# Key sums of a cross-attention kernel: multiply and add in one VectorE operation, eleven of them inside the first layer

## The reference, cut to what matters

```python
x = x + alpha * (softmax((x @ wq.T) @ (ctx @ wk.T).T / sqrt(512)) @ (ctx @ wv.T)) @ wo.T
for i in (1, 2):                                   # the two layers, H=16, K=128
    h  = layer_norm(x, ln_scale[i], ln_offset[i])
    qh = (h @ wq[i] + bq[i]);  kh = (ctx @ wk[i] + bk[i]);  vh = (ctx @ wv[i] + bv[i])
    kh = concat(kh, bias_k[i]);  vh = concat(vh, bias_v[i])   # position 361
    x  = x + softmax(qh @ kh.T / sqrt(128)) @ vh @ wo[i] + bo[i]
h = layer_norm(x, ...);  x = x + gelu(h @ w_fc1 + b_fc1) @ w_fc2 + b_fc2
```

## Time and profile before

| what | value |
|---|---|
| median of 3 runs | 1841.67 us (1839.01 to 1846.27) |
| the profiled execution | 1845.13 us |
| its span, first to last instruction | 1843.3 us |
| mean granted TensorE clock | 0.995 of full |
| busy: PE, DVE, ACT, POOL | 98%, 61%, 44%, 42% of the span |
| DMA | 123.80 MB, mean 67 GB/s |

### The profile page before, as it was taken

The page is one execution under the profiler, slowest core; times in us unless marked ns, Lnnn a source line. Parts: engine busy times, 40 slices in busy tenths (PEclk is TensorE's granted clock), DMA queues, the critical chain, the costliest instruction groups (busy, mean ns, idle before and its releaser), DMA issues.

```text
span 1843.3 us, 30698 instructions
## 1 busy us (share of the span) xinstructions
PE 1814.3 (98%) x11548; PEld 1777.6 (96%) x11548; DVE 1119.8 (61%) x2518; ACT 806.2 (44%) x1868; POOL 773.3 (42%) x634
## 2 busy tenths in 40 slices
PE   8889999999999999999999999999999999999999
PEld 5789999999999999999999999999999999999999
DVE  3676556555575565566688555556666566555565
ACT  3534344434444434344475443444435334434354
POOL 2685252453162352531378245343245252353244
PEclk9999999999999999999999999999999999999999
DMA  8952011111020121210372112121112021111132
GB/s 249 241 172 63 29 53 41 47 58 41 12 76 24 47 59 34 64 31 29 109 227 85 39 47 58 30 58 41 30 52 59 24 62 31 47 58 41 35 100 85
DMA packets 73590, 123.80 MB, mean 67 GB/s; under 512 B 13888, under 2 KB 25536, under 8 KB 73444
## 3 DMA queue, kind: packets, MB, share of 16 engines
q1 hardware_dynamic: 71140, 117.64, 21.8%
q10 hardware_dynamic: 2304, 4.20, 0.7%
HBM read 119.20 MB, written 2.61 MB: 66 GB/s over the span
## 4 chain that ended last, share of the span: by engine, by line
PE 89%; DVE 5%; DMA 2%; ACT 2%; SPq 1%; issue 1%; DVEq 0%; ACTq 0%
PE psum L589 27%; PE psum L590 27%; PE psum L591 27%; PE psum L875 4%; DMA ctxT_in<-ctxT_dram 1%; DVE xT L1536 1%; DMA ctx_rows_in<-ctx_dram 1%; PE psum L750 1%; PE psum L841 1%; DVE h_lo L1342 1%; PE psum L602 1%; PE psum L598 1%; DVE psum L1504 1%; PE psum L599 0%; PE psum L768 0%
## 5 line engine op out<-in xcount | busy, mean ns | idle before, releaser
L471 POOL TENSOR_TENSOR wbuf_hi<-stage,zero_col 128x512 fp32r<-128x512 f32 x256 | 267.5, 1045 | 916.1 <-PE psum L591 545.2
L521 POOL TENSOR_TENSOR wbuf_lo<-stage,wbuf_hi 128x512 fp32r<-128x512 f32 x256 | 329.5, 1287 | 20.1
L589 PE MATMUL psum<-pT_hi,ctx_rows_hi 121*128 121x250 f32 (+3 forms) x1152 | 332.0, 288 | 1.2 <-DVE pT_lo L1338 1.2
L591 PE MATMUL psum<-pT_hi,ctx_rows_lo 121*128 121x250 f32 (+3 forms) x1152 | 332.3, 288 | 0.0
L590 PE MATMUL psum<-pT_lo,ctx_rows_hi 121*128 121x250 f32 (+3 forms) x1152 | 331.1, 287 | 0.0
L589 PE MATMUL psum<-ctxT_hi,a_hi 128*125 128x362 f32 (+1 forms) x832 | 280.5, 337 | 0.0
L1338 DVE TENSOR_TENSOR a_lo<-psum,a_hi 128x500 fp32r<-128x500 f32 (+2 forms) x288 | 146.2, 526 | 210.2 <-ACT a_hi L996 209.5
L591 PE MATMUL psum<-ctxT_hi,a_lo 128*125 128x362 f32 (+1 forms) x832 | 273.2, 328 | 0.0
L590 PE MATMUL psum<-ctxT_lo,a_hi 128*125 128x362 f32 (+1 forms) x832 | 272.9, 328 | 0.0
L589 PE MATMUL psum<-a_hi,wbuf_hi 128*128 128x400 f32 x720 | 254.0, 353 | 0.0
L590 PE MATMUL psum<-a_lo,wbuf_hi 128*128 128x400 f32 x720 | 248.4, 345 | 0.0
(11 more groups left out here) (183 smaller groups left out, 3563.8 us busy)
## 6 DMA issues: line engine op xcount, KB each, us to landing
stage<-head_w_dram SPq DMA_DIRECT2D x256, 256.0 KB, 2.6
mlp_stage<-mlp_w_dram SPq DMA_DIRECT2D x32, 512.0 KB, 3.9
ctx_rows_in<-ctx_dram SPq DMA_DIRECT2D x12, 726.0 KB
ctxT_in<-ctxT_dram SPq DMA_DIRECT2D x12, 724.0 KB, 10.3
key_stage<-head_w_dram SPq DMA_DIRECT2D x32, 256.0 KB, 7.4
l0w<-l_w_dram ACTq DMA_DIRECT2D x16, 256.0 KB, 8.4
kb<-diff_scratch SPq DMA_DIRECT2D x32, 64.0 KB, 4.3
out_dram<-y_out SPq DMA_DIRECT2D x8, 200.0 KB, 2.6
```

Of the source, the lines that this page charges most:

```text
L471: return nc.gpsimd.tensor_tensor(out, in_, zero_col[0:in_.shape[0], :].broadcast_to(tuple(in_.shape)), ALU.add)
L521: nc.gpsimd.tensor_tensor(lo, held, hi.bitcast(F32), ALU.subtract).then_inc(stage_free, 1)
L589: pe.matmul(out, a_h, x_hi, start=start, stop=False)
L591: return pe.matmul(out, a_l, x_hi, start=False, stop=stop)
```

## The change

- A key sum is now four `tensor_tensor_reduce` on DVE, one for each 128 columns, straight from `key_stage` and `kb` (product and sum in one operation). POOL's products and the `kw` buffers are gone.
- Twenty-one sums are done in the single head. The other eleven are done inside steps (0,0) to (1,3) of pass 0, in slot a or b (`LATE_KEYS_AT`), through one pair of buffers, `kb_late` and `key_stage_late`. Their loads stand in SP's list behind the stage loads 8, 12, 14, 15, 17 and 21 (`LATE_KEYS_BEHIND`), and each waits until the sum before it is done.
- `key_parts(0)` stands between centring and inverting of the first norm, where four sums stood; `key_parts(1)` moves from step (0,0) to behind step (3,2).
- The first four pairs of buffers lie over the rows that the `dv_scratch` stores read, so SP waits for `dv_out` before it loads the first keys, and it loads them ahead of `load_ctx_columns(1, 0)`.
- ACT does `exp0(0)` and `exp0(1)` ahead of the splits beside them, and the splits of the context rows of turn 1 come later; DVE does `maxima0(1)` and `maxima0(2)` earlier.
- POOL splits weights 0 to 3 as soon as the 21 sums are done, and clears `dv3`, `pb3` then.

```diff
+KEYS, EARLY_KEYS, KEY_WBUF = 7, 4, 2
+LATE_KEYS_AT = {
+    (0, 0): "b", (0, 1): "ab", (0, 2): "ab", (0, 3): "ab", (1, 0): "b", (1, 1): "b", (1, 2): "b", (1, 3): "b",
+}
+LATE_KEYS_BEHIND = {8: 1, 12: 1, 14: 2, 15: 5, 17: 1, 21: 1}
...
             sp.wait_ge(diff_out, 16)
+            sp.wait_ge(dv_out, 32)
+            some_key_weights(EARLY_KEYS)
             for b in range(3):
                 sp.wait_ge(ls_mm, b + 1)
-                if b == 0:
-                    some_key_weights(4)
                 load_ctx_columns(1, b)
-            some_key_weights(1)
...
-                some_key_weights((2, 2, 1, 5)[b])
+                some_key_weights((1, 2, 1, 2)[b])
...
+                if i < KEYS_BEFORE:
...
+                else:
+                    sp.wait_ge(kw_sum, i)
+                    sp.dma_start(kb_late[:, :], diff_d[i].partition_broadcast(P)).then_inc(late_ld, 16)
+                    sp.dma_start(key_stage_late[:, :], head_w_d[i * 4 + KINDS.index("q")]).then_inc(late_ld, 16)
...
             def key_sums(i):
-                dve.wait_ge(kw_s, i + 1)
-                nc.vector.tensor_reduce(w0[:, :, i], kw[i % len(kw)][:, :, :], AX_X, ALU.add).then_inc(kw_sum, 1)
...
+                for c in range(DC):
+                    summed = nc.vector.tensor_tensor_reduce(
+                        out=chunk(held, c), in0=chunk(held, c), in1=diffs[:, :], scale=1.0, scalar=0.0, op0=ALU.mult,
+                        op1=ALU.add, accum_out=w0[:, c, i:i + 1])
+                summed.then_inc(kw_sum, 1)
...
                 if j == 0:
-                    some_key_sums(4)
+                    key_parts(0)
...
-                        if ph == 0 and before is None:
-                            key_parts(1)
                         run_pieces((k, b, "a"))
+                        if ph == 0 and "a" in LATE_KEYS_AT.get((k, b), ""):
+                            some_key_sums(1)
...
+                    if ph == 0:
+                        some_key_sums("b" in LATE_KEYS_AT.get((k, b), ""))
+                        if (k, b) == (3, 2):
+                            key_parts(1)
```

More of the change, by code:

```diff
@@ L215, in build @@
         dv3 = sb("dv3", [65, 2, 2 * P], F32R)
+        with ExitStack() as before_aside:
+            key_stage_late = sb("key_stage_late", [P, D], F32, before_aside)
+            kb_late = sb("kb_late", [P, P], F32, before_aside)
         aside_hi, aside_lo = split("aside", [P, N])
         with ExitStack() as before_layers:
-            key_stage = sb("key_stage", [P, KEYS, D], F32, before_layers)
+            sb("first_wbufs", [P, KEY_WBUF * 2 * D], F32, before_layers)
+            key_stage += [sb(f"key_stage{j}", [P, D], F32, before_layers) for j in range(EARLY_KEYS, KEYS)]
+        kb = kb_first + kb
         w_hi, w_lo = zip(*[split(f"wbuf{j}", [P, D]) for j in range(WBUFS)])
@@ L551, in _ @@
                             pool.wait_ge(n_lo, n_chunks(BETWEEN, 0, DC - 1))
+                        if ph == 0 and i == KEY_WBUF:
+                            pool.wait_ge(kw_sum, max(k for k in range(KEYS_BEFORE) if k % KEYS >= EARLY_KEYS) + 1)
                         if ph == 0 and i == WBUFS - 1:
-                            pool.wait_ge(kw_sum, LAYERS * H)
+                            pool.wait_ge(kw_sum, KEYS_BEFORE)
                             pool.wait_ge(dv_out, 32)
@@ L1080, in single_head @@
                 exp0(3)
+                ctx_rows_hi(0, 3)
                 queries1_hi(0)
@@ L1171, in queries_hi @@
                 def queries_hi(h):
+                    if ph == 0 and h == ASIDE[0]:
+                        act.wait_ge(kw_sum, LAYERS * H)
                     nc.scalar.activation(made_queries(h)[0], made("q", h), ACT.Identity, bias=bias_of(BQ, h))\
@@ L1355, in key_sums @@
             def key_sums(i):
-                dve.wait_ge(kw_s, i + 1)
-                nc.vector.tensor_reduce(w0[:, :, i], kw[i % len(kw)][:, :, :], AX_X, ALU.add).then_inc(kw_sum, 1)
+                if i < KEYS_BEFORE:
+                    dve.wait_ge(kb_ld[i % KEYS], i // KEYS * 32 + 32)
+                    held, diffs = key_stage[i % KEYS], kb[i % KEYS]
+                else:
+                    dve.wait_ge(late_ld, (i - KEYS_BEFORE) * 32 + 32)
+                    held, diffs = key_stage_late, kb_late
+                for c in range(DC):
[3 more added lines that the diff above has]
+                summed.then_inc(kw_sum, 1)
             keys = iter(range(LAYERS * H))
@@ L1440, in single_head @@
                 maxima0(3)
+                probs0_lo(1)
                 some_key_sums(1)
-                probs0_lo(1)
                 queries1_lo(0)
@@ L1467, in single_head @@
                 residual(0, 0)
+                probs0_lo(4)
                 ctx_columns_lo(1, 3)
-                probs0_lo(4)
                 some_key_sums(1)
```

86 lines of the change are left out of this document (31 added, 55 removed).

## The result

| kernel | median of 8 runs | lowest to highest |
|---|---|---|
| before | 1840.51 us | 1839.01 to 1846.27 |
| changed | 1850.55 us | 1848.77 to 1851.52 |

The ratio is 1.0050, 95% interval 1.0038 to 1.0062: the change costs 10 us. The forecast was 1835.1, between 1827 and 1845: the time lies above the range.

The account below looks back on a forecast made before the run. PE, in flight 98% of the span, was taken as the bound, with gains only ahead of 168 us. Head 2.0, norm 6.2, step (0,0) 3.4, late sums -5.0 gave 6.6 us off 1841.67: 1835.1 us, range 1827 to 1845.

Parts of the forecast that it names:

- Head: Single head, up to the first norm: earlier first exponential, partly handed back; 2 us won, from -3 to +4.
- the price of a key sum: DVE's four product-and-sum operations per key: 1.3 us a sum, bounds 0.68 and 2.2 us.
- The rule that it did weigh: Skill's DVE page: scalar-tensor-tensor with two non-bf16 SBUF sources runs at half throughput; a sum would be 1.8 us.
- slow sums: Rival on DVE's key sums: at 2.2 us a sum the kernel is slower, 1844 us; chance 0.10.
- half pace: Rival on DVE's key sums: half pace in the accumulating form alone, 1.8 us a sum, 1839.4 us; chance 0.10.
- The head starves: Rival: waiting for `dv_out` empties the queues, context lands 5 us later, head -3, total 1840 us; chance 0.15.
- First norm: First norm, up to k0: earlier inverting, faster `h_lo`, no lower clock; 6.2 us won, from 3.8 to 7.
- Step (0,0): Without `key_parts(1)` there, PE's 2.21 us wait falls to 0.5 and the clock holds; 3.4 us won, from 1.5.
- Late sums: Eleven sums inside layer steps: loads come late and PE waits, mainly in steps (0,1) to (0,3); 5 us lost, 3 to 9.
- The chain through q4: Step (0,1): key 23's load waits through stage load 14 and split 12 for PE's q4; PE then waits 2.3 us.
- five forecast waits: PE waits from late sums: 2.3 us at `attend(0,1)`, 1.7 at `probs_lo(0,2,0)`, then 0.3, 0.5 and 0.3.
- The base: Starting point of the sum: profiled execution of 1845.13 us, less 3.46 us to the median of three, 1841.67.

Follow-up runs that it names:

- r_before: The kernel before, unchanged, run again for a second profiled execution: median 1839.36 us.
- e_one: Changed kernel with each 128-column operation of a key sum replaced by a plain one-input sum, without the product: 1838.25 us, ratio 0.999.
- e_load: Changed kernel with key 23's load behind stage load 13 instead of 14: 1845.06 us, ratio 1.003.
- e_full: Changed kernel with two head sums moved, key 23's load one place earlier, ACT's row splits (1,0), (1,1) back, key 30 in slot a: 1838.35 us.
- e_best: Changed kernel, eight head sums moved later, key 23's load earlier, key 30 in slot a, ACT's row splits back, probs0_hi(4) before ctx_columns_hi(1,3): 1838.26 us.
- e_thirds: Changed kernel with each POOL split of context rows issued as three instructions instead of one: 1852.40 us, ratio 1.006.

## Why the prediction was wrong, point by point

- **Head: forecast 2 us won, 8.2 lost (6.3 against the first profile).** The first exponential brought its wait of 1.8 us, and PE was 3.8 us ahead of r_before at `outputs(0,0)` (77.51 against 81.33). The failed step is the price of a key sum: it was taken from undisturbed rows, as one number with an upper bound of 2.2 us, and the sum went by that number wherever a sum stood; a meeting with POOL was put at nothing. The undisturbed price was even too high (0.9, not 1.3; no row stood behind the 0.05 for the accumulator's read, which takes 0.08 and overlaps); beside POOL's splits it was 8.2. Rows that showed the meeting were there. The prediction itself won 2.2 us in the norm by keeping `h_lo` away from POOL's weight splits, and took `key_parts(0)` at 0.45 us where `key_parts(1)` beside such splits took 2.3; it did not carry this over to the new operation. `ctxT_lo` at 2.44 us beside POOL's 2.72 at 86 us was not read. The Trainium skill, "SBUF — State Buffer", section "Who interferes with whom", says that a DVE instruction with two SBUF inputs contends with a GpSimd instruction that reads SBUF, over ports that are an exclusive lock, and that `tensor_reduce` never contends on trn2. The traces agree with both (3.5 us held beside a split; 0 of 128 held in e_one), and the prediction had weighed another page instead.
- **The rule that it did weigh** (half pace with two SBUF sources and an accumulator) is not borne out: 128 columns take 0.28 us with the accumulator and two inputs and 0.28 without in e_one. The rivals "slow sums" and "half pace" had the right sign of mechanism, a dearer sum, and the wrong place: the price is not per sum but per meeting.
- **"The head starves": not in this execution.** `dv_out` let SP go at 49.50, not 54.9, and the new context columns were split on ACT at 59.95, in r_before at 61.06. Their forecast landing at 62.5 was 2.6 us late. That was luck of the execution: in other kernels with the same wait SP went at up to 55.78 and ACT stood for the columns (see the end).
- **First norm: forecast 6.2, measured 6.2 against the first profile and 5.4 against the second.** k0 starts 14.05 us behind the centring (129.59), forecast 13.9, against 20.27 and 19.41 before; `h_lo` takes 1.43 us both times, `key_parts(0)` 0.45, and no lower clock is left. Each link came out as worked.
- **Step (0,0): forecast 3.4, measured 3.4 against the first profile, 1.5 against the second.** The wait fell from 2.21 to 0.38 as said. The half of a spell of clock was an accident of the one execution.
- **Late sums: forecast 5 lost (3 to 9), measured 7.9.** The chain through q4 held: DVE stood 6.29 us for key 23's pair, and PE waited 3.21 at `attend(0,1)` (forecast 2.3). Three things were off. The pair landed 5.0 us behind the split that releases it (175.5 to 180.5), not 3.6: SP took longer over the issues, and each such transfer took 3.3 us or more from issue to landing, where 2.6 had been read from the `stage` loads. "A lower clock in this stretch would mostly run under these waits" was false: the spell of 181.5 to 188.3 outlasted the wait by 5.7 us, and of the 5.9 us that e_load won in this stage 2.7 are not the wait. And of the five forecast waits only the first came, since a sum took 0.9 us; in their stead stood 1.38 at 245.56, another meeting of a key sum with POOL.
- **The base.** The sum was made against an execution 4.6 us above its kernel's median. Two of its three clock spells, which the forecast meant to win back (3.4 and 1.7 us), were not there in the second. Taking 3.46 us off both sides does not undo that, since part of the surplus was counted as won. With the mis-sized head (+8.2 for -2.0), the late sums (7.9 for 5.0) and the spells of that execution (norm 5.4 for 6.2, step (0,0) 1.5 for 3.4) the sum is +9.3 and not -6.6.

## What to carry to other kernels

Before work is moved between DVE and POOL, or fused on DVE, count the SBUF inputs of the new operation: with two it can be held for the length of every two-input POOL instruction that it meets, once for each of its pieces. So price such an operation by its place, look in the trace for the rows where the two engines overlap, and put short two-input operations where POOL is idle. A wait that ends on a load in a chain of one buffer is cheaply cured by one place in the loading order; and before clock spells are counted as gains, a second profile should show them too.

## What was not expected of the hardware

- DVE and POOL alternate strictly, instruction by instruction, when both have such work waiting: a 0.28 us chunk took 3.49 to 3.56 us beside splits of 3.5, and 1.35 to 1.38 beside splits of 1.2. POOL loses less: of the three splits from 83.94 on, two took 3.5 us, and the one that met `ctxT_lo` (1.66 us alone) took 4.9.
- Operations with two inputs are not the only kind that is held. `pb<-pT_lo`, a cast, and `prob<-prob,stats`, a product with a column, read one tensor from SBUF. In the changed kernel all 12 of the casts that began beside POOL's splits were held (0.75 to 1.36 us instead of 0.28), and 6 of 12 of the products (up to 1.10 instead of 0.41); in the kernel before it was 12 of 12 and some of the products too. None of 247 additions of a PSUM tensor to `xT` was, and no `TENSOR_REDUCE`. So one input is safe in the reductions seen here, not in general. DVE and POOL in the changed kernel:

```profile
243.95 1.07 DVE L1609 TENSOR_SCALAR prob<-prob,stats 125x362 f32<-125x362 f32 x1
```

```profile
243.78 1.04 POOL L491 TENSOR_TENSOR wbuf_hi<-stage,zero_col 128x512 fp32r<-128x512 f32 x1 [1.76 <-PE psum L587]
```

- The clock does not fall at each pause of PE of this size. It fell behind or during waits of 1.93, 2.21, 2.38 and 3.21 us, and of 1.79 in e_full, and not behind 1.77 and 1.41 in r_before nor behind 2.76, 1.76 and 3.18 in e_one, whose granted clock was 1.000 throughout. No run here says what decides it.
- The same head code starts its second turn at different times, and in the changed kernels the start follows the landing of the second `dv_scratch` transfer, since SP's wait for `dv_out` holds back all later loads. It landed at 47.3 us in e_best, 49.4 in the changed kernel and 55.7 in e_thirds. In the six executions with 50.3 or later ACT then stood 1.9 to 6.1 us for the first new context columns. ACT in e_thirds:

```profile
67.34 1.41 ACT L994 ACTIVATE ctxT_hi<-ctxT_in 128x1448 fp32r<-128x1448 f32 x1 [6.14 <-DMA ctxT_in<-ctxT_dram]
```

Counted from that landing, the head takes 58.0 and 58.2 us in the changed kernel and e_load, 55.8 in e_thirds, 50.3 to 52.1 in the four with two sums moved, 49.8 in e_one, and 46.6 to 48.1 in the three with the stretch clear. That is nearly the order of how much is held; e_one, whose rows of the context landed late, stands out. Without this correction, heads of single profiles can't be compared closer than 3 us. Why the landing moves stays open, and no run tried the change without the wait for `dv_out`.
